# The shared expert's first half: downs as rounded products, rows behind two groups, scatters in two counts

## The reference

```python
x = x + tanh(g_xattn) * attention(layernorm(x), ctx)          # 16 heads
xf = layernorm(x)                                             # 2048 tokens x 256
logits = xf @ Wg                                              # 16 experts
topi = top_k(logits, 2); gates = softmax over the two
for e in range(16):
    h = silu(xf @ W1[e] + b1[e]) * (xf @ W11[e] + b11[e])     # 512 wide
    y = y + (h @ W2[e] + b2[e]) * gates[:, e]
z = silu(xf @ Ws1 + bs1) * (xf @ Ws11 + bs11) @ Ws2 + bs2     # shared, 1024 wide
x = x + tanh(g_ffn) * (y + z)
```

## Time and profile before

| | |
|---|---|
| median of 3 runs | 568.99 us (568.74 to 569.06) |
| the profiled execution | 574.73 us, span 572.6 us |
| mean granted clock of PE | 0.997 |
| busy: PE / PEld | 546.3 us (95%) / 440.9 us (77%) |
| busy: DVE / ACT / POOL | 353.6 / 238.5 / 333.2 us |
| DMA | 76.08 MB, mean 133 GB/s |

### The profile page before, as it was taken

One profiled execution on the slowest core, in us unless ns is written; L12 is line 12 of the kernel. 1 busy time (PEld: TensorE's weight loads), 2 busy tenths in 40 slices (PEclk: granted clock), 3 DMA queues, 4 the chain that ended last, 5 costly groups with the idle time before them and its releaser, 6 DMA issues.

```text
span 572.6 us, 12049 instructions
## 1 busy us (share of the span) xinstructions
PE 546.3 (95%) x3290; PEld 440.9 (77%) x3291; DVE 353.6 (62%) x861; ACT 238.5 (42%) x788; POOL 333.2 (58%) x273
## 2 busy tenths in 40 slices
PE   7889999999979999988999999999999999999996
PEld 6556667666758878777888888888888888888785
DVE  5757788787678732345665566555665556435677
ACT  1899999999994201202222122221222212232232
POOL 4689999998863486623364674444444830236550
PEclk8999999999999999999999999999999999999999
DMA  8571001000112144335458777656665210113332
GB/s 284 245 300 64 21 20 38 29 26 20 65 39 103 46 166 174 105 98 185 140 177 293 249 287 259 201 201 211 211 211 201 82 46 29 35 54 107 109 111 73
DMA packets 32899, 76.08 MB, mean 133 GB/s; under 512 B 4961, under 2 KB 21857, under 8 KB 29921
## 3 DMA queue, kind: packets, MB, share of 16 engines
q1 hardware_dynamic: 14960, 52.44, 25.5%
q10 hardware_dynamic: 14832, 14.82, 8.0%
q0 software_dynamic: 3072, 8.39, 4.7%
HBM read 54.93 MB, written 18.61 MB: 128 GB/s over the span
## 4 chain that ended last, share of the span: by engine, by line
PE 80%; DVE 8%; issue 5%; another core or an unknown queue 3%; ACT 2%; POOL 2%; DVEq 0%; ACTq 0%; POOLq 0%
PE mid L749 14%; PE big L730 8%; PE big L731 8%; PE big L732 7%; PE big L517 5%; PE big L653 4%; PE mid L740 4%; PE big L651 3%; PE big L652 3%; PE mid L530 3%; PE work L549 3%; PE last L670 2%; PE work L670 2%; PE last L542 2%
## 5 line engine op out<-in xcount | busy, mean ns | idle before, releaser
L939 ACT ACTIVATE last<-arena 128x512 f32<-128x512 f32 x47 | 28.3, 602 | 183.3 <-DVE arena L1409 183.3
L837 ACT ACTIVATE arena<-big,nmax 128x128 f32<-128x128 f32 x256 | 90.7, 404 | 9.0 <-DVE nmax L1061 8.4
L749 PE MATMUL mid<-dring,arena 128*128 x376 | 88.9, 379 | 0.0
L1409 DVE TENSOR_TENSOR arena<-big,bring 128x512 f32<-128x512 f32 x47 | 32.5, 692 | 87.2 <-PE big L732 87.2
L730 PE MATMUL big<-u_hi,xsT_hi 128*128 x188 | 81.8, 435 | 1.6 <-issue 1.6
L1572 POOL TENSOR_TENSOR u_lo<-arena,u_hi 128x2048 fp32r<-128x2048 f32 x16 | 74.4, 4652 | 1.3
L749 PEld LDWEIGHTS mid<-dring,arena 128*128 128x128 f32 x376 | 67.8, 190 | 7.4
L732 PE MATMUL big<-u_hi,xsT_lo 128*128 x188 | 73.5, 391 | 0.0
L731 PE MATMUL big<-u_lo,xsT_hi 128*128 x188 | 73.4, 390 | 0.0
L1548 POOL TENSOR_TENSOR arena<-arena,rinv 128x1024 f32<-128x1024 f32 (+1 forms) x32 | 58.7, 1834 | 13.3 <-DVE rinv L1069 13.0
L1672 POOL TENSOR_TENSOR pool_mark<-mhalf 128x1 f32<-128x1 f32 x15 | 2.9, 194 | 104.0 <-PE big L732 87.6
(11 more groups left out here) (198 smaller groups left out, 1202.9 us busy)
## 6 DMA issues: line engine op xcount, KB each, us to landing
arena<-up_w_dram SPq DMA_DIRECT2D x16, 1024.0 KB, 7.6
bring<-expert_bias_dram SPq DMA_DIRECT2D x16, 640.0 KB
dring<-down_w_dram SPq DMA_DIRECT2D x18, 512.0 KB
sorted_y<-arena ACTq DMA_DIRECT2D x47, 128.0 KB, 1.7
arena<-sorted_x ACTq DMA_DIRECT2D x43, 128.0 KB, 2.1
sorted_x<-dring SPq DMA_DIRECT2D x3, 1536.0 KB, 9.4
arena<-ctx_t_dram ACTq DMA_DIRECT2D x8, 256.0 KB, 2.8
dring<-up_w_dram SPq DMA_DIRECT2D x2, 1024.0 KB, 4.8
```

Source lines behind the costliest of these rows:

```text
L749: i = mm(mid[:, 1, 0:D], gT[:, p, c, :], dring[:, slot, c * D:(c + 1) * D], start=(c == 0), stop=(c == HC - 1))
L837: i = nc.scalar.activation(probs[:, u % 2, h, :], big[:, u % 2, h // 4, (h % 4) * CTX:(h % 4 + 1) * CTX], ACT.Exp, bias=nmax[:, u % 2, h:h ...
L1409: v.tensor_tensor(hb1[:, p, :], big[:, p, 0, :], bring[:, slot, 0:HID], ALU.add).then_inc(h1_ready, 1)
```

## The change

- The first half's downs become rounded products by chunks, in the code of the second half: `shared_down(n)` serves both halves, with four banks (`first_bank`) for the first half too. Down n − 2 follows up n, from group 2 on; before that the lag is three chunks.
- ACT rounds the first half's down weights (`first_d`), DVE keeps their remainder; ACT and DVE also round each of the first half's 16 hidden chunks (`round_hidden`, `keep_rest`). The hidden chunk goes through `gg`, its two parts lie in `first_gs`; both new tensors take space of the arena that the attention has left.
- Totals and ranks of the router use other columns of `mid`, and down 0 waits until they have been read.
- The last pair's `xfT` is rounded by ACT and DVE, no longer by POOL between scatters.
- The first two blocks' rows are transposed into `big` behind downs 13 and 14, ahead of down 15; the last downs no longer stand between block 0 and block 1.
- The scatters count on two semaphores, for pairs of tiles in turn; the issue of a pair waits only for the pair before the last one, and nothing waits in POOL behind the last.

```diff
+        first_d = sb("first_d", [P, 2, DCOLS], F32R)
+        first_gs = sb("first_gs", [P, 2, 2, 512], F32R)
...
+        first_bank = (work, last, mid[:, 0, :], mid[:, 1, :])
+        def hidden_chunk(n):
+            return gg[:, n % 2, :] if n < HC * TILES // GROUP else gshT[:, n // HC % 2, n % HC, :]
+        def rounded_chunk(n):
+            if n < HC * TILES // GROUP:
+                return first_gs[:, 0, n % 2, :], first_gs[:, 1, n % 2, :]
+            return gs_hi[:, n % 2, :], gs_lo[:, n % 2, :]
...
-            def shared_down(s, tiles=range(GROUP)):
-                for t in tiles:
-                    if n >= 2:
-                        pe.wait_ge(z_taken, n - 1)
-                    for c in range(HC):
-                        i = mm(zbank[t % 2][:, 0:D], gshT[:, s % 2, c, t * P:(t + 1) * P], dring[:, slot, c * D:(c + 1) * D],
...
+            def shared_down(n):
+                pe.wait_ge(gs_lo_ready, n + 1)
+                if n == 0:
+                    pe.wait_ge(d_split, 1)
+                    pe.wait_ge(lg_taken, PAIRS)
+                    pe.wait_ge(rank_taken, 1)
...
+                for t in range(GROUP):
+                    if c == 0 and h > 0:
+                        pe.wait_ge(z_taken, GROUP * (h - 1) + t + 1)
+                    mm(banks[t][:, 0:D], g_hi, w_hi, start=(c == 0), stop=False)
+                    mm(banks[t][:, 0:D], g_hi, w_lo, start=False, stop=False)
+                    i = mm(banks[t][:, 0:D], g_lo, w_hi, start=False, stop=(c == HC - 1))
...
             shared_up(0, 3)
+            shared_down(0)
             pe.wait_ge(xfT_kept, 4)
-            shared_up(1, 0)
...
+            for n in range(4, 8):
+                shared_up(1, n - 4)
+                shared_down(n - 3)
+            shared_down(5)
             pe.wait_ge(xfT_kept, PAIRS)
+            for n in range(8, 15):
+                shared_up(n // HC, n % HC)
+                shared_down(n - 2)
...
-            transpose_rows(0, 0)
-            shared_down(3, range(1))
-            transpose_rows(1, 1)
+            shared_up(3, 3)
+            shared_down(13)
+            shared_down(14)
+            transpose_rows(0, 0, big[:, 0, 0, :])
+            transpose_rows(1, 1, big[:, 0, 1, :])
+            shared_down(15)
+            pe.wait_ge(xsT_ready, 2)
+            pe.wait_ge(gsh_ready, HC * TILES // GROUP)
             up(0, 0)
-            pe.wait_ge(xsT_ready, 2)
-            shared_down(3, range(1, GROUP))
-            pe.wait_ge(z_taken, 4 * GROUP)
+            pe.wait_ge(z_taken, TILES)
             transpose_rows(2, 2)
...
+            act.wait_ge(w_even, 32)
+            nc.scalar.activation(first_d[:, 0, :], dring[:, 0, :], ACT.Copy).then_inc(d_hi_done, 1)
+            round_hidden(0)
+            act.wait_ge(xfT_ready, PAIRS)
+            nc.scalar.activation(xfT_hi[:, :, 2 * P * LAST:2 * P * PAIRS], xfT[:, :, :], ACT.Copy).then_inc(xfT_hi_kept, 1)
...
+            for n in range(8, 16):
+                shared_silu(n // HC, n % HC)
+                round_hidden(n)
...
+            keep_rest(0)
+            dve.wait_ge(d_hi_done, 1)
+            v.tensor_tensor(first_d[:, 1, :], dring[:, 0, :], first_d[:, 0, :], ALU.subtract).then_inc(d_split, 1)
             shared_hidden(0, [2])
...
+            for n in range(8, 15):
+                shared_hidden(n // HC, [n % HC])
+                if n % HC == 1:
+                    add_shared(n // HC - 1)
+                keep_rest(n)
+            shared_hidden(3, [3])
+            keep_rest(15)
+            copy_rows(0, 0, big[:, 0, 0, :])
+            copy_rows(1, 1, big[:, 0, 1, :])
+            add_shared(3)
...
             for t in range(TILES):
+                landed = scattered_odd if t // 2 % 2 else scattered_even
+                if t >= 4 and t % 2 == 0:
+                    pool.wait_ge(landed, 16 * TOPK * 2 * (t // 4))
                 for k in range(TOPK):
                     g.indirect_dma_start(...)
-                if t == GROUP - 1:
-                    keep_xfT(LAST)
-                if t % GROUP == GROUP - 1:
-                    pool.wait_ge(scattered, 16 * TOPK * (t + 1))
```

More of the change, by code:

```diff
@@ L148, in flamingo_layer @@
         ARENA = 16128
-        arena = sb("arena", [P, ARENA])
+        with nc.sbuf_tensor("arena", [P, ARENA], F32) as whole:
+            arena = whole
+        first_d = sb("first_d", [P, 2, DCOLS], F32R)
+        first_gs = sb("first_gs", [P, 2, 2, 512], F32R)
+        sb("arena_rest", [P, ARENA - 2 * DCOLS - 4 * 512])
         taken = [0]
@@ L354, in chunk_used @@
             if c == HC - 1:
-                engine.wait_ge(z_ps, TILES + GROUP * (h + 1))
+                engine.wait_ge(z_ps, GROUP * (h + 1))
             else:
@@ L791, in _ @@
             down(BLOCKS - 1, (BLOCKS - 1) % 2)
[L793 to L813, removed]
             for n in range(2, 4 * HC):
                 shared_up(4 + n // HC, n % HC)
-                last_down(n - 2)
-            last_down(4 * HC - 2)
-            last_down(4 * HC - 1)
+                shared_down(14 + n)
+            shared_down(8 * HC - 2)
+            shared_down(8 * HC - 1)
         @block.scalar
@@ L925, in shared_silu, with round_hidden @@
                     .then_inc(silu_ready, 1)
-            for s in range(4):
-                for c in range(HC):
-                    shared_silu(s, c)
+            def round_hidden(n):
+                act.wait_ge(gsh_ready, n + 1)
+                if n >= 2:
+                    chunk_used(act, n - 2)
+                nc.scalar.activation(rounded_chunk(n)[0], hidden_chunk(n), ACT.Copy).then_inc(gs_hi_ready, 1)
+            shared_silu(0, 0)
+            act.wait_ge(w_even, 32)
[3 more added lines that the diff above has]
+            nc.scalar.activation(xfT_hi[:, :, 2 * P * LAST:2 * P * PAIRS], xfT[:, :, :], ACT.Copy).then_inc(xfT_hi_kept, 1)
+            shared_silu(0, 1)
+            round_hidden(1)
+            shared_silu(0, 2)
+            for n in range(3, 8):
+                shared_silu(n // HC, n % HC)
+                round_hidden(n - 1)
+            round_hidden(7)
+            for n in range(8, 16):
+                shared_silu(n // HC, n % HC)
+                round_hidden(n)
             act.wait_ge(gate_exp_in, 1)
@@ L1288, in _, with copy_rows @@
             pair(LAST, 1, False, True, False)
-            def copy_rows(b, p):
+            def copy_rows(b, p, bank=work):
                 dve.wait_ge(xs_ps, b + 1)
@@ L1354, in _ @@
             dve.wait_ge(rank_ps, 1)
-            v.scalar_tensor_tensor(out=cnt[:, 0, :], in0=starts, scalar=float(P), in1=mid[:, 0, 0:E], op0=ALU.mult, op1=ALU.add) \
+            v.scalar_tensor_tensor(out=cnt[:, 0, :], in0=starts, scalar=float(P), in1=mid[:, 0, D:D + E], op0=ALU.mult, op1=ALU.add) \
                 .then_inc(rank_taken, 1)
@@ L1378, in _ @@
             next_lo(0)
[L1379 to L1382 removed]
+            shared_hidden(1, [1])
+            keep_rest(4)
+            next_lo(1)
+            next_lo(2)
+            shared_hidden(1, [2])
+            next_lo(3).then_inc(split_done, 1)
             dve.wait_ge(w_even, 32)
             add_shared(0)
[L1385 to L1391 removed]
+            keep_rest(5)
+            shared_hidden(1, [3])
+            keep_rest(6)
+            keep_rest(7)
+            for n in range(8, 15):
[8 more added lines that the diff above has]
+            add_shared(3)
             dve.wait_ge(gate_exp, 1)
@@ L1437, in _ @@
             add_biases(0, 0)
-            add_shared(3, range(1, GROUP))
             copy_rows(2, 0)
```

125 lines of the change are left out of this document (58 added, 67 removed).

## The result

The changed kernel takes 591.21 us (median of 4 runs, 589.88 to 592.27), the kernel before beside it 569.02: a ratio of 1.0384 (95% interval 1.0362 to 1.0406), 22.2 us more where 4.8 less were forecast. The profiled execution took 590.52 us, its span 588.8.

A forecast was written before the change was run, and what follows sets the result against it. TensorE was taken as the bound: 8.6 us saved before block 2, less 3.8 for POOL's split coming first, gain 4.8; 568.99 − 4.8 = 564.2 us, range 559.4 to 568.8.

The forecast's parts named there:

- The downs: Shared expert's first half on TensorE: each down takes 1.43 us instead of 1.73, sixteen 22.9 instead of 27.7, gain 4.8.
- the hole before down 0: TensorE waits for DVE's chain ending in `rank_taken`, which comes 1.1 us later; a hole of 0.8 us.
- The scatters: POOL's 32 issues take 39.3 us at 1.27 each, plus 0.8 for slow early ones; last issued at 233.4.
- this edit buys nothing by itself: Removing POOL's scatter waits gains nothing alone; it only keeps the scatters off the path.
- Rival 2: TensorE's completions reach ACT and DVE some 2.5 us late, at bank changes and blocks 0 and 1; 571.2 us, chance 0.09.
- forecast stretch: TensorE from up chunk 4 to block 2: 65.2 us against 73.80, before 3.8 is given back to POOL's split.
- POOL's split first: POOL's subtraction for expert 2 starts before DVE's last remainder, which waits for it; 3.8 us TensorE hole, held likelier.
- rival 1: DVE's last remainder starts before POOL's subtraction, so the whole 8.6 us gain stays; 560.4 us, chance 0.30.
- The rest of the sum: Other TensorE pieces up to block 2: ups, transposes, register loads 0.8 and waits about 0.3, within the 65.2 us.
- Rival 3: Scatters slow beside busier DVE, from about 1.6 us each, and rows arrive last; 569.1 us, chance 0.09.
- the gain given back later: Sign of the forecast being wrong altogether: TensorE idle between 280 and 480 us, in the expert blocks.

The follow-up runs named there:

- e1: The changed kernel, with POOL again waiting after every four tiles (8 scatters) until all scatters so far have landed; 565.36 us, 0.9916 of the kernel before.
- e2: The kernel before with only the scatters' two counts and pair waits put in, its wait at every fourth tile taken out; 589.44 us, 1.0343.
- e4: The kernel before, unchanged, run again for a second profile; 568.56 us.
- e3: e1 with POOL's split of expert 2's weights also waiting for DVE's last remainder; 566.02 us, 0.9939 of the kernel before.
- e10: e3 once more with more rounds, in the same sitting as e9; 566.89 us, 0.9906 of the kernel before.
- e12: The kernel of e3 in a third sitting; 566.11 us beside 569.38 for the kernel before, 0.9940.
- e14: The kernel of e3 run beside e13 on the same chip; 566.95 us, 0.9904 of the kernel before.
- e13: e3 with POOL's split moved further, behind DVE's four small gate operations; 563.98 us beside 572.60 for the kernel before, 0.9850.
- e9: e1 once more with more rounds; 570.54 us beside 572.61 for the kernel before, 0.9954.
- e5: The changed kernel with SP's two loads of down weights moved behind the loads of rows, after the scatters; 590.21 us, 1.0373 of the kernel before.
- e6: The changed kernel with twelve tiny POOL operations after every eighth scatter, no wait for landings; 568.47 us, 0.9996 of the kernel before.

## Why the prediction was wrong

**The downs: right.** 12 products run from 197.66 to 199.09, 1.43 us. The wide subtraction took 1.22 us (1.15 taken), and the hole before down 0 is 0.8 (188.43 to 189.24).

**The scatters: the step that failed.** Their pace was right to 1 us: no wait bound, and from the first issue to the last it took 41.1 us (191.52 to 232.61) where 40.1 were forecast, 39.3 and 0.8. The slow early issues were read too small: in the kernel before the first four intervals are 1.1 us over 1.27 each. That the last came at 232.61, 0.8 ahead of the forecast 233.4, is no merit of the sum: the changed kernel's profile runs 1.7 us ahead of the one that I forecast from (188.43 against 190.14). But "this edit buys nothing by itself" is wrong. Between the changed kernel and e1 nothing differs but these waits, and between them lie 1.0384 and 0.9916 or 0.9954, 4.3 to 4.7%, some 25 us; in the kernel before the same edit costs 3.4% (e2), 19.5 us. I priced the waits by who was waiting, POOL, and took the pause in its issuing for pure loss. So the step that failed is the price of these waits, put at nothing for TensorE: the pause was what kept TensorE's completions moving.

**Rival 2: the right mechanism, much too small, and argued away by the wrong fact.** I gave it 0.09 and 2.2 us. Against it I put that the late ones "lie within the scatters, which now end earlier". They lie there because of the scatters, and ending them earlier meant issuing them without a pause. Its price took every completion 2.5 us late, as in the earlier trace rows; the delay is no constant but builds up with unbroken issues, to 24.0 us. And it spoke of what waits for TensorE alone: that TensorE's own issue stops as well was not in it.

The size follows from the rows. From 213.31 to 237.52 TensorE did 11 products of an up and 12 of a down, 4.0 us of work at their usual spacing, in 24.2: 20.2 lost. Behind it eight products of an up stood 0.43 apart instead of 0.23 at the lower clock, and after the second hole the last down and block 0's first products lost 1.9 likewise: 3.5 together. That is 23.7 over the forecast stretch of 69.0; measured are 92.95 (188.43, the end of up chunk 3, to block 2 at 281.38), 24.0 over it. The first product of block 2:

```profile
281.38 0.49 PE L758 MATMUL big<-u_hi,xsT_hi 128*128 x1 [0.59 <-issue]
```

The Trainium skill ("Perfetto Trace Analysis", section "Per-engine timelines") says that a TensorE record's end is estimated, and that the completion is sent when the accumulator's memory has acknowledged the writes and is seen by the others later still, both outside the record. The trace agrees that a record's end is not the completion: 211.81 against 229.46.

**POOL's split first: right.** The remainder was forecast at "some 5 us" and took 4.97, the hole 3.93 for 3.8. Its order came out as argued, by 0.10 us. But the order decides less than I made of it. The slow subtraction of the earlier trace rows, DVE's row first below and POOL's second, began 0.58 us ahead of POOL's elementwise work and still ended 0.56 behind it; e2 and e4 show the same.

```profile
202.61 2.19 DVE L1376 TENSOR_TENSOR u_lo<-dring,u_hi 128x512 fp32r<-128x512 f32 x1
```
```profile
203.19 1.05 POOL L1555 TENSOR_TENSOR xfT_hi<-xfT,const 128x512 fp32r<-128x512 f32 x1
```

So it is not shown that the 8.6 us of rival 1 would have stayed with DVE first by a hair; no run has that order for the last remainder. What I missed as well is that taking the split out of the way moves the collision to the next DVE operation in line (e3), down to one of 128x16. The Trainium skill ("SBUF — State Buffer", section "Who interferes with whom") has this too: `tensor_scalar` can enter the two-port mode that contends with GpSimd, when its operands meet the mode's conditions. The runs agree: 3.10 to 3.30 us beside POOL (e3, e10, e12 and e14), 0.18 alone (e13).

**The rest of the sum: 2 us too good in this stretch.** With the waits back, the stretch is 71.1 us in e1 (69.0 forecast with one collision, and e1 has two) and 67.1 in e13 (65.2 without). Two pieces are seen in e13: 0.5 us of waiting at a late completion before down 14, and 1.5 before block 0 where 0.8 was counted. Against the second profile of the kernel before (72.1) that is 1.0 and 5.0 us; the timed runs gave 2.1 to 4.5 and 8.6. Where that difference lies is open: late completions vary from run to run, the clock dips in some profiles (for 6.8 us about block 0 in e9, nowhere near it in e1) and one profile is one run.

**Rival 3** did not occur in the changed kernel; the last rows were loaded long before TensorE asked for them. TensorE idle between 280 and 480 us, which would have shown the gain given back later, did not occur either (199.41 of 200).

**What stays open** is how POOL's issue reaches TensorE's completions. Late packets are not it: in e5, which stalls like the changed kernel, the scatters' packets begin about 1.5 us after each issue, before the stall and in it, as most do in the kernel before. Nor is a starved instruction stream seen: the two queues that carry instructions moved one packet each from 190 to 240 us, in the kernel before as in the changed one. That the completions come out in POOL's pauses is only roughly so: in e6 a rounding on ACT that had waited for TensorE went at 214.04, 0.7 us before a pause began.

## What to carry to other kernels

A wait that costs its own engine time can be what keeps another going: before removing a pause from a row of indirect DMAs, look for waits that name no engine while the row runs, and ask when they end. In this kernel rows of eight with a pause of some 2 us kept the loss small, and rows of four removed it while TensorE had to hand over work beside them; each pause also puts off the moment when all rows are there. When a DVE instruction is moved out of POOL's way, look at the next DVE instruction that will stand in its place.

## What was not expected of the hardware

- Indirect DMAs issued by POOL without a pause, one every 1.27 us, delay TensorE's completions, from about the thirteenth on, by up to 24.0 us, and then hold TensorE's instructions 0.7 to 2.1 us apart, with no wait in its program.
- ACT and DVE show none of it among themselves: in the same stretch of the changed kernel DVE's remainder of chunk 7 begins 0.67 us after ACT's rounding (216.18 to 216.85), as elsewhere.
- The granted clock fell to its lower level within the first hole, at 220.5 us, stayed there until 241.0, 3.5 us into the full work after it, and fell again within the 3.9 us hole, at 268.3, for 6.8 us.
